# TensorE's order in the routing stage of a graph, linear-attention and expert layer: where the identity products that bring x stand

## The reference

```python
xn = _layernorm(x)                                    # x is 12500 x 256
x = x + gnn(xn, [src, dst]) + mix(xn)                 # rest of the chain left out
# gnn, per node n, 4 heads:  alpha = softmax(leaky_relu(a_l[src[n]] + a_r[dst[n]]))
#   out = sum_h alpha[h] * (xn @ weight)[dst[n], h]
# mix: q, k = elu(.) + 1;  context = k^T v;  D_inv = 1 / max(q . k_sum, 1e-6)
#   out = (q @ context * D_inv) @ Wproj^T + bproj     # 8 heads of 32
x = x + ffn(_layernorm(x))
# ffn: logits = h @ gate_w + gate_b; idx = argmax; pos = running count of idx - 1
#   tokens with pos < C go to expert idx: relu(h w1 + b1) w2 + b2, times the probability
```

## Time and profile before

| | us |
|---|---|
| median of 3 runs | 1488.85 (1488.57 to 1491.13) |
| the profiled execution | 1488.98 |
| its span, first to last instruction | 1487.1 |
| middle stage, from TensorE's first product to its last listing | 359.9 to 715.3 |

### The profile page before, as it was taken

The page is one execution under the profiler, slowest core; times in us unless marked ns, Lnnn a source line. Parts: engine busy times, 40 slices in busy tenths (PEclk is TensorE's granted clock), DMA queues, the critical chain, the costliest instruction groups (busy, mean ns, idle before and its releaser), DMA issues.

```text
span 1487.1 us, 30487 instructions
## 1 busy us (share of the span) xinstructions
PE 1390.6 (94%) x9008; PEld 1245.1 (84%) x9008; DVE 1130.4 (76%) x2919; ACT 906.1 (61%) x2045; POOL 690.7 (46%) x604
## 2 busy tenths in 40 slices
PE   6999999998989889887599999999999999999995
PEld 5999999997777777776399999999999999999995
DVE  6888888884698888898556867678677776777765
ACT  3545554553376666676467667676676766757663
POOL 1211001112788878875506454464554544545534
PEclk9999999998799999999699999999999999999998
DMA  4444334432444544456111211223122231212001
GB/s 99 79 89 78 86 74 89 88 76 67 96 121 119 127 126 126 118 129 183 41 58 47 68 29 25 81 50 96 41 58 66 53 91 41 76 41 52 7 15 20
DMA packets 131134, 112.46 MB, mean 76 GB/s; under 512 B 69068, under 2 KB 116877, under 8 KB 130936
## 3 DMA queue, kind: packets, MB, share of 16 engines
q1 hardware_dynamic: 78196, 72.83, 19.7%
q0 software_dynamic: 52864, 38.82, 11.8%
HBM read 76.17 MB, written 43.85 MB: 81 GB/s over the span
## 4 chain that ended last, share of the span: by engine, by line
PE 50%; issue 0%; DVE 0%; POOL 0%; POOLq 0%; ACT 0%; DVEq 0%; ACTq 0%
PE psY L1767 24%; PE psH L1790 24%; PE psX L1741 2%; POOL out L1482 0%; POOLq L1289 0%; ACT q_all L1537 0%; DVE q_all L1717 0%; DVE q_all L1728 0%; DVE q_all L1730 0%; DVE q_all L1666 0%; DVE q_all L1723 0%; DVE fin L1719 0%; DVE q_all L1715 0%; POOLq L1482 0%; DVEq L35 0%
## 5 line engine op out<-in xcount | busy, mean ns | idle before, releaser
L1684 DVE TENSOR_TENSOR h_lo<-q_all,h_hi 128x496 fp32r<-128x496 f32 x256 | 173.0, 676 | 197.6 <-PE psY L1767 87.0
L1463 POOL DMA_INDIRECT out<-q_all,to_i x124 | 173.5, 1399 | 311.5 <-issue 286.7
L1551 ACT ACTIVATE h_hi<-psH,b_sb 128x496 fp32r<-128x496 f32 x256 | 172.4, 673 | 232.1 <-PE psH L1790 222.3
L1767 PE MATMUL psY<-w_hi,h_hi 128*124 128x256 f32 x1024 | 289.2, 282 | 0.0
L1767 PE MATMUL psY<-w_hi,h_lo 128*124 128x256 f32 x1024 | 287.1, 280 | 0.0
L1767 PE MATMUL psY<-w_lo,h_hi 128*124 128x256 f32 x1024 | 286.8, 280 | 0.0
L1767 PEld LDWEIGHTS psY<-w_lo,h_hi 128*124 128x124 f32 x1024 | 188.9, 184 | 8.9
L1767 PEld LDWEIGHTS psY<-w_hi,h_hi 128*124 128x124 f32 x1024 | 188.8, 184 | 8.0
L1767 PEld LDWEIGHTS psY<-w_hi,h_lo 128*124 128x124 f32 x1024 | 189.1, 185 | 0.0
L1446 POOL DMA_INDIRECT q_all<-out,from_i x112 | 163.5, 1460 | 54.6 <-issue 54.6
L1553 ACT ACTIVATE q_all<-psH,b_sb 128x496 f32<-128x496 f32 x256 | 170.7, 667 | 0.0
(11 more groups left out here) (257 smaller groups left out, 3215.3 us busy)
## 6 DMA issues: line engine op xcount, KB each, us to landing
x_sb<-in_x SPq DMA_DIRECT2D x50, 448.0 KB
q_all<-in_L_ffn_w SPq DMA_DIRECT2D x16, 1024.0 KB, 7.4
graph_table<-tab_sb SPq DMA_DIRECT2D x25, 511.0 KB
out<-xd SPq DMA_DIRECT2D x25, 448.0 KB
x_sb<-in_x SPq DMA_DIRECT2D x50, 52.0 KB
out<-q_all,to_i POOLq DMA_INDIRECT x128, 4.3
q_all<-out,from_i POOLq DMA_INDIRECT x112, 4.7
graph_table<-tab_sb SPq DMA_DIRECT2D x25, 59.3 KB
```

The costliest lines, as they stand in the source:

```text
L1463: pool.indirect_dma_start(out=out, in_=o_sb[:, par, j, :], in_offset=None, out_offset=bass.IndirectOffsetOnAxis(ap=to_i[:, par, j:j + 1], ...
L1551: act.activation(h_hi[:, f % 4, :], psH[f % 2][:, 0:TS3], ACT.Relu, bias=b1_sb[:, bass.ds(e * NF + f, 1)]).then_inc(s_hhi_ready, 1)
L1684: nc.vector.tensor_tensor(h_lo[:, f % 4, :], hf[:, f % 4, :], h_hi[:, f % 4, :].bitcast(F32), ALU.subtract).then_inc(s_hlo_ready, 1)
L1767: ins = nc.tensor.matmul(psY[par][j // 2][0:T3, (j % 2) * D:(j % 2 + 1) * D], hh[:, f % 4, j * T3:(j + 1) * T3], w[:, f, :], start=f == 0 ...
```

## The change

The call of `x_part(s + 1)` moves from the head of TensorE's step to the place between the fourth listing product and `positions(s)`. Nothing is added or removed, the other four engines' programs are the same row for row, and the waits inside `x_part` go with it.

```diff
 def step(s, par, h, ahead):
     first = isinstance(s, int) and s == 0
-    if ahead > 0:
-        x_part(s + 1, 1 - par, h + par + 1)
     if not first:
         listed(s - 1, range(J - 1), False)
     if ahead > 2:
         q_ksum(s + 3, s + 2)
     if ahead > 1:
         inverse(s + 2)
     if not first:
         listed(s - 1, range(J - 1, J), False)
+    if ahead > 0:
+        x_part(s + 1, 1 - par, h + par + 1)
     positions(s, ahead)
     if ahead > 0:
         mix(s + 1)
     if ahead > 1:
         den_spread(s + 2)
```

## The result

The changed kernel takes 1544.08 us (median of 4 runs, 1536.52 to 1546.75) against 1488.73 of the kernel before: ratio 1.0352, 95% interval 1.0329 to 1.0375. Slower, as forecast, but by 55 us instead of 33, and above the range of 1500 to 1539. The profiled execution took 1541.67, its span 1539.9.

What follows compares the result with a forecast made beforehand. VectorE was taken to set the step at full clock, TensorE to end last only when its clock falls. 1488.98 us + 30.4 (falls less waits for the mix) + 3.4 (step 0) = 1522.8, given as 1522, range 1500 to 1539.

Steps and rivals of the forecast that it cites:

- What bounds a step at full clock: Middle stage: VectorE sets the step of 12.6 to 13.2 us, TensorE's order lies under it, so the move costs 0 us.
- step 0: First step: denominators wait for `den`, then run with the identity products at the low clock, delaying `positions`: +3.4 us.
- The slack of 0.3 us: TensorE ahead of `positions`, full clock: identity products end 0.3 us before `oh_sum` lets `positions` start, where slack was 0.87.
- Where falls meet the step: Low clock moves from the mix to denominators, listing and identity products, all ahead of `positions`, so `picked` pays.
- The price of a fall: Low clock ahead of `positions`: 1.5 us for one low stretch, 3.2 for both denominators and identity products, middle 2.35.
- The number of falls: Middle stage: falls go by the thin stretch's length, 3.7 us growing to 5.3, so 15 of 23 steps.
- the credit of 4.9 us: VectorE ahead of `xd`: its 4.9 us of waiting for the mix mostly go, as the low stretch ends before the mix.
- The rival of wide work ahead of the mix: Identity products just ahead of the mix shield it, the clock no longer falls there: faster, 1484 us; chance 0.06.

Runs made afterwards that it cites:

- the second trace: The changed kernel itself, run again beside the kernel before on another chip of the first kind: 1540.27 us, ratio 1.0332.
- x_behind_inverse: Changed kernel with the identity products one place earlier, between the inverse and the fourth listing; only on the second kind of chip: ratios 0.9844 and 0.9893.
- the half move: Against the kernel before, the identity products moved behind the three listings but ahead of the denominators: 1487.96 us, ratio 0.9981.

## Why the prediction was off

**What bounds a step at full clock: right.** TensorE's order costs nothing there. With the three wide products the clock is at 1.00, the order is the changed one, and the ratio to before is 0.9992, step 0 included: its 23 steps take 296.6 us against 299.9, which makes up for its step 0 of 25.0 us against 21.5. The slack of 0.3 us ahead of the positions was nearer to nothing, though: in that trace TensorE is idle there for at most 0.14 us in steps 1 to 23. It cost nothing that shows, since `picked` waits 3.6 us in all behind step 0, against 3.3 in the kernel before.

**Where falls meet the step: right.** They lie over denominators, fourth listing and identity products; the mix is at full level in 22 of 24 steps; VectorE's idle moved from `xd` to `picked`.

**The price of a fall: right.** The prediction had 1.5 us for one low stretch, 3.2 for two, and 2.35 as the middle. The steps measure 14.6 and 16.1 us; from the 12.9 of steps at full clock (296.6 / 23, with three wide products) that is 1.7 and 3.2.

**The number of falls: this is the step that failed.** I put 15 of 23 by going with the length of the thin stretch, 11 x 5.3 / 3.7. There is one in each of the 23 steps (21 in the second trace). With 23, the same sum gives 23 x 2.35 - 4.9 = 49.2, and the traces differ by 49.5. That it comes so near is partly luck. Against the 296.6 us of full clock the kernel after is 52.8 us longer, 2.30 a fall instead of 2.35, and the kernel before 3.3 us longer, not 4.9; the two differences nearly cancel. The proportion was wrong: from 3.7 us of thin stretch to 5.3, 43% more by the forecast (5.66 us in the first step shown, 437.42 to 443.08), the count went from 10 to 23 of 23. The 5.3 us are also of another kind than the 3.7: they hold the denominators and the gaps between single listings, with no run of wide products from the spreading to their end. Which of the two, length or kind, makes the count isn't shown; x_behind_inverse was to tell and met the second kind of chip. The runs with one and three wide products show how steep it is: 1540, 1503, 1490.

**The range.** It let the price vary and held the count at 15 or below, so nothing in it stood for more falls. Its two ends were also not worked out alike: the upper one, 15 x 3.2 = 48, left out the credit of 4.9 us, and the lower one, 1507, left out the 3.4 of step 0.

**Step 0: right.** 24.9 us from its `xd` to the next against 21.5, +3.4. The denominators of tile 3 took 3.50 us at the low level (0.50 from 394 to 401.3) and the identity products 3.73, and the positions started at 401.26 (forecast 400.6; the whole step began 0.7 us later than before).

**The credit of 4.9 us: right as a wait, less as time.** The wait for the mix fell by 4.0 to 0.9 us; what the falls of the kernel before cost its 23 steps was 3.3 us, by the sum above.

**The rival of wide work ahead of the mix** was right in one part, that the mix is hardly met any more (at full level in 22 of 24 steps), and wrong in that the falls did not go but came elsewhere. Idle time in the stretch doesn't explain them: with thin products in every gap TensorE was busy 98% of the time (379.82 of 386.69 us) and the clock was at 0.80.

## What to carry to other kernels

Before moving wide matmuls out of a queue's gap, ask what remains around the narrow ones: here short products, single listings and small waits stood in one piece (5.66 us in the first step shown, 437.42 to 443.08, TensorE busy for 4.56 of it), and a fall from 1.00 to 0.50 came in each of the 23 steps of the first trace and in 21 of the second. Put the wide products next to the narrow ones (the half move, 9 falls and 1487.96 us), and if nothing useful is at hand, a product that nobody reads can pay for itself (three a step took 51 us off the changed kernel, which brought it back to the time of the kernel before), as long as it stands where the engine waits anyway. And read a fall's price from what lies behind it: over the mix, with 1.5 us of cover, steps with one low stretch took 12.1 to 13.3 us, as those without, and the two with a stretch twice as long 14.4; ahead of the positions, with next to no cover, it cost 1.7 or 3.2.

## What was not expected of the hardware

The same kernel differs by 6% from chip to chip, or from one occasion to the other: 1488 to 1491 us on some, 1573 to 1588 on others. There ScalarE starts on a TensorE transpose behind the narrow products 5.59 us after the end of its record (in the lines above), where elsewhere it starts 0.12 us after. The sign of this change may depend on it: the changed order itself was not run there, but the kernels nearest to it are 1.1 to 1.6% faster.

With narrow products in every gap TensorE was busy 98% of the time and its clock was at 0.80; three wide products in their place, 0.44 us each where the thin ones took 0.78, held it at 1.00.
